# Query and key transfers split by groups of four heads, values from plain fp32, and a new order, in a transformer layer on one core

## The chip, the cores and the metric

The kernel runs on one core of one Trainium2 chip. The time is in device microseconds of one launch. The kernel before was timed in three runs: median 1072.35 us, 1069.49 to 1074.19.

A core has a matrix engine (PE, TensorE), a vector engine (DVE), a scalar engine (ACT) and GpSimd (POOL). Each works through its own list of instructions in order. SP (SyncE) computes nothing and issues transfers (DMAs). The engines wait for each other only by semaphores: an instruction that waits holds everything behind it on its engine.

## The reference

One layer of a vision tower on 8 images of 1024 tokens. 29 features are embedded into 128 channels and a table of positions is added. Then follow a layer norm, causal attention with 8 heads of 16 channels and a residual, and a second layer norm with a feed-forward part: a shared one and eight experts in two groups, of which each token takes two.

```python
def _L0_attn_ref(x, Wq, bq, Wk, bk, Wv, bv, Wo, bo):
    ...
    Q = split_heads(x @ Wq + bq)
    K = split_heads(x @ Wk + bk)
    V = split_heads(x @ Wv + bv)
    scores = jnp.einsum('bhqd,bhkd->bhqk', Q, K)
    causal = jnp.tril(jnp.ones((n, n), dtype=jnp.float32))
    mask = (1.0 - causal) * -100000.0
    attn = jax.nn.softmax((scores + mask) / math.sqrt(d), axis=-1)
    out = jnp.einsum('bhqk,bhkd->bhqd', attn, V)
    out = out.transpose(0, 2, 1, 3).reshape(b, n, c)
    return out @ Wo + bo
...
h = _L0_tok_ref(x, L0_tok_W)
h = h + _L0_attn_ref(_layernorm(h, axis=-1), ...)
h = h + _L0_ffn_ref(_layernorm(h, axis=-1), ...)
```

## The kernel before

**Split numbers.** Most fp32 products are made from a rounded part (`_h`, type fp32r) and its rest (`_l`), as three matmuls with fp32r operands: h*h, l*h and h*l (`split_mm`, L501 to L503). Some are plain fp32 matmuls, which the trace shows as two records each: embedding (L519), output projection (L623), gates (L633), and the weighing of the values (L598).

**Halves, units, passes.** An image has two halves of 512 tokens. The front of a half is: `emb` (embedding, then positions added by DVE), `stat1` (statistics on DVE and POOL), `turn1` (z turned by PE, L527; ACT copies the rounded part, `ztl` is DVE's subtraction), `q`, `k`, `v` (projections; ACT rounds, DVE subtracts, L747). All of these use one PSUM bank, `bank_m`.

Attention runs in four units of an image, (heads 0-3, half 0), (heads 4-7, half 0), (heads 0-3, half 1), (heads 4-7, half 1). Pass 1 makes every score (`score`, L553) and DVE takes row maxima from it (L767, L771). `turn` turns the maxima of a unit, DVE splits them and SP puts them as two more rows beside the queries (L470). Pass 2 (`prob`, L580) makes the scores again, the other way round and less the maximum; ACT takes the exponential (L1025), and `weigh` (L598) multiplies with the values. Scores and probs have two PSUM banks each.

**The stacks.** So that one matmul gives all three products of the split numbers, the 16 channels of a head stand three times in the rows of `q_stack` (h, h, l) and `k_stack` (h, l, h). They come there by transfers from SBUF to SBUF on SP's queue: six per half for the queries (L449) and six for the keys (L462), each 128 KB with all eight heads. The rows without channels hold zeros, and the keys' last two rows hold -1, against the maxima. The -1 are put in by eight small transfers at the beginning (`ones`). A half of `q_stack` is used by image after image, so the queries wait until the last `prob` of that half in the image before has been made:

```python
            def queries(i, half):
                sp.wait_ge(m_taken, after(i, "q", half))
                if i:
                    sp.wait_ge(st_ready, ((i - 1) * NP_ + HALF_P[half]) * G4)
```

**The order.** Each engine's list is woven from streams (scores, probs, weighing, middle, forward, combine, transfers) by strings of letters, one letter per step: `FIRST` for the start, `WEAVE` for each of six images in between, `LAST` for the end. In one period an engine makes probs of one image, the forward part of it and of the one before, and fronts and scores of the next. SP has the steps `queries` and `keys` of a half in its list, the maxima of the four units and the stores.

## Time and profile before

| | |
|---|---|
| median of 3 runs | 1072.35 us |
| profiled execution | 1073.58 us |
| its span | 1071.9 us |
| PE busy | 986.7 us (92%) |
| DVE busy | 777.3 us (73%) |
| ACT busy | 591.3 us (55%) |
| POOL busy | 322.1 us (30%) |
| transfers | 35.06 MB |

The span is one execution from its first to its last instruction. Busy time is a mean over stages that differ: at the beginning PE is nearly idle, in the middle it hardly ever is. A busy PE may still be slowed by its clock, which has two levels; the profile gives the granted one as a part of full speed. A time in brackets behind a row of the timeline is idle time of that engine just before, with the instruction or transfer that ended it. "PEld" is PE's loading of weights, which runs beside its matmuls.

### The profile page before, as it was taken

The numbers are of one execution on the slowest core, as the hardware profiler recorded it, in microseconds if no ns is written. First come the engines' busy times: TensorE is split into PE (matmuls) and PEld (weight loads), VectorE is DVE, ScalarE is ACT, GpSimd is POOL, SyncE is SP. The second block draws the span as 40 slices with busy tenths as digits, with TensorE's granted clock in tenths as the row PEclk, the third lists the DMA queues.
The fourth block names the chain that finished last, engine by engine and source line by source line (L and its number), as shares of the span: only waits on it lengthen the run. The fifth ranks groups of instructions, "written<-read, shape, count | busy, mean of one in ns | idle before, by whom it ended". The sixth has DMA issues, their size and how long they took to land.

```text
span 1071.9 us, 17016 instructions
## 1 busy us (share of the span) xinstructions
PE 986.7 (92%) x5552; PEld 665.1 (62%) x5552; DVE 777.3 (73%) x2444; ACT 591.3 (55%) x1351; POOL 322.1 (30%) x466
## 2 busy tenths in 40 slices
PE   2598999999999999999999998999989999899976
PEld 2354556676657666676667666666657676575554
DVE  6478758885788857986688857987588858788233
ACT  2034655566554665557545765647655665446734
POOL 3031313324232223324142333323142242322334
PEclk9999999999999999999999999999999999899989
DMA  3540045003140045002350053100550041300000
GB/s 118 69 56 2 10 53 74 1 2 50 34 63 2 2 72 74 1 2 31 43 73 1 2 72 49 26 1 3 71 72 2 1 64 33 45 2 1 12 1 20
DMA packets 29480, 35.06 MB, mean 33 GB/s; under 512 B 5696, under 2 KB 15936, under 8 KB 29264
## 3 DMA queue, kind: packets, MB, share of 16 engines
q1 hardware_dynamic: 29392, 33.97, 21.5%
q8 instruction: 45, 0.74, 0.3%
q14 instruction: 43, 0.35, 0.1%
HBM read 4.02 MB, written 4.19 MB: 8 GB/s over the span
## 4 chain that ended last, share of the span: by engine, by line
PE 75%; DVE 9%; DMA 4%; ACT 3%; SPq 3%; issue 3%; POOL 2%; ACTq 0%; POOLq 0%; DVEq 0%
PE bank_p L580 14%; PE bank_s L553 13%; PE bank_w L598 11%; PE bank_f L679 5%; PE bank_f L680 5%; PE bank_f L681 5%; DMA q_stack<-qk_l 3%; PE bank_m L645 3%; PE bank_f L501 2%; SPq L449 2%; PE bank_f L503 2%; PE bank_f L502 2%; DVE mx_far L767 2%; PE bank_m L501 2%; ACT pt L1025 1%
## 5 line engine op out<-in xcount | busy, mean ns | idle before, releaser
L1025 ACT ACTIVATE pt<-bank_p 128x512 f32<-128x512 f32 (+3 forms) x768 | 350.0, 491 | 266.0 <-PE bank_p L580 260.6
L553 PE MATMUL bank_s<-k_stack,q_stack 112*128 112x512 f32 (+3 forms) x768 | 273.4, 394 | 36.3 <-DMA q_stack<-qk_l 12.5
L771 DVE CUSTOM_DVE_ANT_0 bank_s<-bank_s,causal 128x384 f32<-128x384 f32 (+3 forms) x512 | 246.0, 507 | 65.2 <-PE bank_s L553 60.7
L580 PE MATMUL bank_p<-q_stack,k_stack 128*128 128x512 f32 (+3 forms) x768 | 256.4, 379 | 5.3 <-ACT pt L1025 4.2
L553 PEld LDWEIGHTS bank_s<-k_stack,q_stack 112*128 112x128 f32 x768 | 146.9, 197 | 140.1 <-DVE mx L771 58.0
L767 DVE TENSOR_REDUCE mx_far<-bank_s 128x1 f32<-128x512 f32 x256 | 166.8, 684 | 35.2 <-PE bank_s L553 33.5
L1166 POOL TENSOR_SCALAR_AFFINE_SELECT pt<-pt 128x512 f32<-128x512 f32 x128 | 81.8, 639 | 361.0 <-ACT pt L1025 361.0
L580 PEld LDWEIGHTS bank_p<-q_stack,k_stack 128*128 128x128 f32 x768 | 138.9, 193 | 77.6 <-ACT pt L1025 48.7
L598 PE MATMUL bank_w<-pt,v 128*32 128x512 f32 (+3 forms) x1536 | 159.3, 497 | 0.6 <-POOL pt L1166 0.5
L679 PE MATMUL bank_f<-wex_h,hid_h 128*128 128x512 f32 x256 | 103.2, 403 | 0.1
L681 PE MATMUL bank_f<-wex_h,hid_l 128*128 128x512 f32 x256 | 101.2, 395 | 0.0
L680 PE MATMUL bank_f<-wex_l,hid_h 128*128 128x512 f32 x256 | 101.2, 395 | 0.0
L1198 POOL TENSOR_TENSOR sel<-sel 128x256 f32<-128x256 f32 x64 | 47.2, 737 | 145.3 <-ACT sel L1087 144.9
L1087 ACT ACTIVATE sel<-sel,wsel 128x128 f32<-128x128 f32 x256 | 81.4, 394 | 12.3 <-DVE sel L935 11.7
L1081 ACT ACTIVATE sel<-bank_f,gm 128x512 f32<-128x512 f32 x64 | 44.1, 688 | 58.6 <-PE bank_f L681 48.4
L771 DVE DVE_READ_ACCUMULATOR2_ANT mx<- 128x1 f32 x512 | 72.6, 142 | 0.0
L935 DVE SCALAR_TENSOR_TENSOR sel<-bank_f,gm,sel 128x512 f32<-128x512 f32 x64 | 47.7, 745 | 30.5 <-PE bank_f L681 27.9
L598 PEld LDWEIGHTS bank_w<-pt,v 128*32 128x32 f32 x1536 | 32.7, 108 | 55.0 <-issue 35.2
L501 PE MATMUL bank_f<-z2t_h,win_h 128*128 128x512 f32 x128 | 54.7, 428 | 2.5 <-DVE gate L916 1.8
L679 PEld LDWEIGHTS bank_f<-wex_h,hid_h 128*128 128x128 f32 x256 | 48.2, 188 | 11.0 <-issue 2.8
L681 PEld LDWEIGHTS bank_f<-wex_h,hid_l 128*128 128x128 f32 x256 | 48.1, 188 | 11.3
L680 PEld LDWEIGHTS bank_f<-wex_l,hid_h 128*128 128x128 f32 x256 | 48.5, 190 | 8.8
(130 smaller groups left out, 1351.5 us busy)
## 6 DMA issues: line engine op xcount, KB each, us to landing
q_stack<-qk_h SPq DMA_DIRECT2D x64, 128.0 KB, 3.9
k_stack<-qk_h SPq DMA_DIRECT2D x64, 128.0 KB, 5.8
q_stack<-qk_l SPq DMA_DIRECT2D x32, 128.0 KB, 5.2
k_stack<-qk_l SPq DMA_DIRECT2D x32, 128.0 KB, 5.9
out<-h SPq DMA_DIRECT2D x16, 256.0 KB, 4.3
x_sb<-x_t SPq DMA_DIRECT2D x16, 64.0 KB, 5.7
pt<-w_expert SPq DMA_DIRECT2D x1, 1024.0 KB, 5.6
pos_sb<-pos SPq DMA_DIRECT2D x2, 256.0 KB, 3.1
```

What stands on the lines that cost most here:

```text
L501: nc.tensor.matmul(dst, wh, xh, start=True, stop=False)
L553: nc.tensor.matmul(s_bank[s % 2][:, 0:cols], q_stack[0:STACK, half, hd, t % HT * P:(t % HT + 1) * P], k_stack[0:STACK, hd // 2, key_place( ...
L580: nc.tensor.matmul(p_bank[p % 2][:, q0:HALF], k_stack[:, hd // 2, key_place(i, kt // HT), kt % HT * P:(kt % HT + 1) * P], q_stack[:, half, ...
L598: mm = nc.tensor.matmul(w_bank[VW * j:VW * (j + 1), q0:HALF], v[:, i % 2, kt, first:first + VW], pt[:, k % PT_SLOTS, j, q0:HALF], start=(k ...
L679: nc.tensor.matmul(f_bank[g][:], hid_h[:, c, tok], wex_h[:, c, w], start=(c == 0), stop=False)
L680: nc.tensor.matmul(f_bank[g][:], hid_h[:, c, tok], wex_l[:, c, w], start=False, stop=False)
L681: mm = nc.tensor.matmul(f_bank[g][:], hid_l[:, c, tok], wex_h[:, c, w], start=False, stop=(c == HID // P - 1))
L767: nc.vector.tensor_reduce(mx_far[:, u, col:col + 1], s_bank[s % 2][:], AX.X, ALU.max).then_inc(s_taken, 1)
L771: nc.vector.tensor_tensor_reduce(src, src, causal[:, HALF - cols:HALF], 1.0, -3.0e38, ALU.add, ALU.max, mx[:, u, col:col + 1]).then_inc(s_ ...
L1025: nc.scalar.activation(pt[:, k % PT_SLOTS, j, q0:HALF], p_bank[p % 2][:, q0:HALF], ACT.Exp, scale=0.25).then_inc(exp_done, 1)
L1087: nc.scalar.mul(sel[:, t % 2, part], sel[:, t % 2, part], wsel[:, t, e:e + 1]).then_inc(weighted, 1)
L1166: nc.gpsimd.affine_select(out=d, in_=d, compare_op=ALU.is_ge, fill=0.0, base=0, pattern=[[0, G4], [1, P]], channel_multiplier=-1).then_inc ...
```

## The change

The change has four parts, and a new set of orders that goes with them.

1. **Transfers by groups.** Queries and keys go to their stacks by groups of four heads: six transfers of 64 KB for each of queries and keys, half and group, so 48 per image and not 24. Each group has its own semaphore, and a score waits for its unit's group alone. A group's queries wait only until the `prob` steps of their own unit in the image before are through (`UNIT_LAST`).
2. **The keys' stack is filled with -1** in all its rows, once, and the queries' stack with zeros; the product of the unused rows stays zero. The eight small transfers go. ACT fills half 0 of the queries and the first place of the keys, POOL the rest.
3. **A shorter beginning.** DVE clears only x_sb (in halves) and mx. Positions are loaded on ACT's queue. Weights of queries and keys come first, those for the output projection and the feed-forward part are loaded behind the first half's stacks (`load_rest`), into other tiles than before (`gate`, `hid`, and no more `pt`). Weights are split behind z.
4. **Values from plain fp32.** ACT also copies the turned z unrounded, back into `z`; one fp32 matmul per tile of 128 tokens takes the place of three. The next half's z waits for them.

```diff
-    moves = [("queries", 0), ("keys", 0), ("queries", 1), ("keys", 1)]
+    moves = [(what, half, g) for half in range(2) for g in range(2) for what in ("queries", "keys")]
 FIRST = {
     "pe": (
-        "mmmmmmmdmssssdsssssmsmsmssmsssmssssssmssmssssssppsspsssppsspspmspsdppsppspswsswppdsswsppspspswss"
...
+        "mmmmmdmmmmmmssdssmmssssssssssssssmsmsssssssssssppsspspssspmspdswspsppsdpssspsppsswppssppspssswss"
...
-            def queries(i, half):
+            def queries(i, half, g):
 
                 sp.wait_ge(m_taken, after(i, "q", half))
                 if i:
-                    sp.wait_ge(st_ready, ((i - 1) * NP_ + HALF_P[half]) * G4)
+                    sp.wait_ge(st_ready, ((i - 1) * NP_ + UNIT_LAST[2 * half + g] + 1) * G4)
                 for n, part in enumerate((qk_h, qk_h, qk_l)):
                     for odd in range(2):
                         to = slice(odd * ODD + n * DH, odd * ODD + (n + 1) * DH)
-                        rows = part[odd * (P // 2):(odd + 1) * (P // 2), 0, :]
-                        sp.dma_start(words(q_stack[to, half, odd::2, :]), words(rows)).then_inc(q_in[half], 16)
+                        sp.dma_start(words(q_stack[to, half, g * G4 + odd:(g + 1) * G4:2, :]),
+                                     group_rows(part, 0, odd, g)).then_inc(q_in[half][g], 16)
...
+                if (i, half, g) == (0, 1, 0):
+                    sp.wait_ge(other_keys_made, 1)
...
                     keys(i, st[1], st[2])
                     if st[2] and i < B - 1:
                         load_x(i + 1, st[1])
+                    if i == 0 and st == ("keys", 0, 1):
+                        load_rest()
...
                 if kind == "v":
...
-                        mm = split_mm(m_bank[:, tok], zt_h[:, tok], zt_l[:, tok], wqkv_h[:, 2, :], wqkv_l[:, 2, :])
+                        mm = nc.tensor.matmul(m_bank[:, tok], z[:, t, :], wv_sb[:], start=True, stop=True)
...
-                if s == UNIT_S0[0] or s == UNIT_S0[2]:
-                    pe.wait_ge(q_in[half], (i + 1) * 96)
-                if s == UNIT_S0[0] or s == UNIT_S0[2] + ROWS:
-                    pe.wait_ge(k_in[half], (i + 1) * 96)
+                if s == UNIT_S0[u]:
+                    pe.wait_ge(q_in[half][g], (i + 1) * 96)
+                if s == UNIT_S0[u] + half * ROWS:
+                    pe.wait_ge(k_in[half][g], (i + 1) * 96)
...
-                        dve.wait_ge(m_ready, after(half_before(i, half)[0], "turn1", 1 - half))
+                        dve.wait_ge(m_ready, after(half_before(i, half)[0], "v", 1 - half))
...
-                dve.wait_ge(zth_made, n + 1)
+                dve.wait_ge(zt_made, n + 1)
...
-            nc.vector.memset(x_sb[XROWS:ODD, :, :], 0.0).then_inc(x_padded, 1)
-            nc.vector.memset(x_sb[ODD:P, :, :], 0.0).then_inc(x_padded, 1)
-            nc.vector.memset(words(k_stack[:, 0:2, :, :]), 0.0).then_inc(keys_zeroed, 1)
-            nc.vector.memset(words(k_stack[:, 2:, :, :]), 0.0).then_inc(stacks_zeroed, 1)
-            nc.vector.memset(words(minus1), -1.0).then_inc(minus1_made, 1)
+            for half in range(2):
+                nc.vector.memset(x_sb[XROWS:ODD, half, :], 0.0).then_inc(x_padded, 1)
+                nc.vector.memset(x_sb[ODD:P, half, :], 0.0).then_inc(x_padded, 1)
...
                     nc.scalar.copy(zt_h[:], m_bank[:]).then_inc(zth_made, 1)
+                    nc.scalar.copy(z[:].rearrange("p t c -> p (t c)"), m_bank[:]).then_inc(zt_made, 1)
...
+                    if i == 0 and st == ("q", 0):
+                        act.wait_ge(blank_made, 2)
+                        nc.scalar.copy(k_stack[:, :, 0, :], blank[:, 1:2].unsqueeze(2).to_broadcast([P, HEADS // 2, HALF])).then_inc(first_keys_made, 1)
...
             def constants():
+                pool.wait_ge(z_made, HT)
...
+                nc.gpsimd.memset(words(k_stack[:, :, 1:3, :]), -1.0).then_inc(other_keys_made, 1)
```

How the lists move, at three places. First DVE at the very beginning, before (`wqkv` are the three projections' weights, `bank_m` is the embedding at its first use):

```order
L983 MEMSET x_sb 32x1024
L984 MEMSET x_sb 64x1024
L985 MEMSET k_stack 128x3072
L986 MEMSET k_stack 128x3072
L987 MEMSET hid_l 2x1024
L988 MEMSET mx 128x512
L718 TENSOR_TENSOR h<-bank_m,pos_sb 128x512
L724 BN_STATS stats<-h 128x6 x4
...
L947 CAST wqkv_h<-z 128x128 x3
L950 TENSOR_TENSOR wqkv_l<-z,wqkv_h 128x128 x3
L736 TENSOR_SCALAR z<-h,mv,rs 128x128 x4
```

and the same of the changed kernel:

```order
L990 MEMSET x_sb 32x512
L991 MEMSET x_sb 64x512
...
L992 MEMSET mx 128x512
L723 TENSOR_TENSOR h<-bank_m,pos_sb 128x512
L729 BN_STATS stats<-h 128x6 x4
...
L741 TENSOR_SCALAR z<-h,mv,rs 128x128 x4
L952 CAST wqk_h<-z 128x128 x2
L955 TENSOR_TENSOR wqk_l<-z,wqk_h 128x128 x2
L747 TENSOR_TENSOR zt_l<-bank_m,zt_h 128x512
```

The two memsets of the keys' stack and the one for the -1 are gone from ahead of h (those of x_sb stand twice), and the weights' split stands behind z.

Second SP where the second half's queries of an image in the middle are sent, before (`mrow` are the rows of maxima, `st_ready` counts probs):

```order
L449 DMA q_stack<-qk_h 16x4x512 [waits st_ready,m_bank_taken]
L449 DMA q_stack<-qk_h 16x4x512 x3
L449 DMA q_stack<-qk_l 16x4x512 x2
L470 DMA q_stack<-mrow_h 1x16x128 [waits m_bank_taken]
L470 DMA q_stack<-mrow_l 1x16x128
L462 DMA k_stack<-qk_h 16x4x512 [waits st_ready,m_bank_taken]
L462 DMA k_stack<-qk_h 16x4x512
L462 DMA k_stack<-qk_l 16x4x512 x2
```

and of the changed kernel, from the same queries on:

```order
L449 DMA q_stack<-qk_h 16x2x512 [waits st_ready,m_bank_taken]
L449 DMA q_stack<-qk_h 16x2x512 x3
L449 DMA q_stack<-qk_l 16x2x512 x2
L474 DMA q_stack<-mrow_h 1x16x128 [waits m_bank_taken]
L474 DMA q_stack<-mrow_l 1x16x128
L474 DMA q_stack<-mrow_h 1x16x128 [waits m_bank_taken]
L474 DMA q_stack<-mrow_l 1x16x128
L465 DMA k_stack<-qk_h 16x2x512 [waits st_ready,m_bank_taken]
L465 DMA k_stack<-qk_h 16x2x512
L465 DMA k_stack<-qk_l 16x2x512 x2
```

The maxima of units 0 and 1 now both stand ahead of the half's first keys, and behind these (not shown) follow the second group's queries and keys.

Third PE at the beginning, from the first values' projection on, before (`bank_s` holds scores):

```order
L501 MATMUL bank_m<-wqkv_h,zt_h 128x128 [waits m_bank_taken]
L502 MATMUL bank_m<-wqkv_h,zt_l 128x128
L503 MATMUL bank_m<-wqkv_l,zt_h 128x128
...
L553 MATMUL bank_s<-k_stack,q_stack 128x128 [waits keys_in_stack_0,queries_in_stack_0]
...
L553 MATMUL bank_s<-k_stack,q_stack 128x256 [waits scores_taken] x4
L553 MATMUL bank_s<-k_stack,q_stack 128x384 [waits scores_taken] x2
```

and of the changed kernel:

```order
L544 MATMUL bank_m<-wv_sb,z 128x128 [waits m_bank_taken,w_values_loaded]
L544 MATMUL bank_m<-wv_sb,z 128x128 x3
L531 MATMUL bank_m<-ident,z 128x128 [waits m_bank_taken,z_made]
...
L559 MATMUL bank_s<-k_stack,q_stack 128x128 [waits keys_in_stack_0_0,queries_in_stack_0_0]
...
L505 MATMUL bank_m<-zt_h,wqk_h 128x512 [waits m_bank_taken]
...
L559 MATMUL bank_s<-k_stack,q_stack 128x256 [waits scores_taken] x4
```

Four matmuls stand for the twelve of the values, the second half's z is turned ahead of the first score, and its projections follow the first four scores.

## Rows read from the trace of the kernel before

**Rows 1.** Busy time by stretch: start, length, busy us per engine, clock, DMA.

```profile
30.00:40.00 10.00, 1.61 (x8) 1.42 (x7) 2.97 (x13) 0.00 (x0) 1.28 (x2) 1.00 0.98 113
...
426.10:549.00 122.90, 119.38 (x696) 81.67 (x695) 95.12 (x306) 72.97 (x169) 38.38 (x56) 0.99 0.23 33
```

**Rows 2.** PE's waits: instruction, releaser, us in total, times, longest.

```profile
PE bank_s L553 <- DMA q_stack<-qk_l: 12.5, 7, 2.7
...
PE bank_s L553 <- DMA k_stack<-qk_h: 8.7, 1, 8.7
```

**Rows 3.** Timeline of the beginning: start, us, engine, line, operation, [idle before].

```profile
3.30 2.04 PE L519 MATMUL bank_m<-tokw_sb,x_sb 128*128 128x128 f32 x8 [3.30 <-DVE x_sb L984]
...
3.85 2.62 DVE L985 MEMSET k_stack<- 128x3072 f32 x1 [0.70 <-issue]
...
11.21 0.62 DVE L718 TENSOR_TENSOR h<-bank_m,pos_sb 128x512 f32<-128x512 f32 x1
...
14.74 3.01 DVE L947 CAST wqkv_h<-z 128x128 fp32r<-128x128 f32 x3
...
18.49 1.10 DVE L736 TENSOR_SCALAR z<-h,mv,rs 128x128 f32<-128x128 f32 x4
...
25.49 2.60 SPq L449 DMA_DIRECT2D q_stack<-qk_h  x4
...
31.99 1.25 SPq L462 DMA_DIRECT2D k_stack<-qk_h  x2
...
40.31 0.66 PE L553 MATMUL bank_s<-k_stack,q_stack 112*128 112x128 f32 x2 [8.70 <-DMA k_stack<-qk_h]
```

**Rows 4.** Timeline where images change: queries' rest, last prob, transfers, wait, score.

```profile
404.88 0.75 DVE L747 SCALAR_TENSOR_TENSOR qk_l<-bank_m,bq_sb,qk_h 128x512 fp32r<-128x512 f32 x1
...
413.54 0.34 PE L580 MATMUL bank_p<-q_stack,k_stack 128*128 128x128 f32 x2
...
413.95 2.47 SPq L449 DMA_DIRECT2D q_stack<-qk_h  x4
...
416.47 1.24 SPq L449 DMA_DIRECT2D q_stack<-qk_l  x2
...
420.66 0.33 PE L566 MATMUL bank_m<-ident,mx 128*128 128x128 f32 x1
...
422.83 0.94 PE L553 MATMUL bank_s<-k_stack,q_stack 112*128 112x512 f32 x2 [1.84 <-DMA q_stack<-qk_l]
```

**Rows 5.** Timeline of PE, the same wait in three later images.

```profile
545.50 0.77 PE L553 MATMUL bank_s<-k_stack,q_stack 112*128 112x512 f32 x2 [1.59 <-DMA q_stack<-qk_l]
...
791.89 0.73 PE L553 MATMUL bank_s<-k_stack,q_stack 112*128 112x512 f32 x2 [1.64 <-DMA q_stack<-qk_l]
...
913.97 0.73 PE L553 MATMUL bank_s<-k_stack,q_stack 112*128 112x512 f32 x2 [1.98 <-DMA q_stack<-qk_l]
```

**Rows 6.** Busy time by stretch, just behind two of these waits.

```profile
423.00:425.00 2.00, 2.00 (x7) 1.22 (x8) 1.29 (x2) 0.38 (x1) 1.33 (x3) 0.55 1.07 127
...
792.00:794.00 2.00, 1.89 (x10) 1.25 (x10) 1.50 (x3) 0.65 (x2) 1.60 (x3) 1.00 1.09 125
```

**Rows 7.** Timeline of PE: one half's values, one half's embedding, and what follows each.

```profile
369.40 1.05 PE L519 MATMUL bank_m<-tokw_sb,x_sb 128*128 128x128 f32 x8
...
370.21 0.54 PE L580 MATMUL bank_p<-q_stack,k_stack 128*128 128x384 f32 x2
...
383.45 0.33 PE L501 MATMUL bank_m<-wqkv_h,zt_h 128*128 128x128 f32 x1
...
384.85 0.67 PE L580 MATMUL bank_p<-q_stack,k_stack 128*128 128x512 f32 x2
```

**Rows 8.** Groups of instructions: count, busy us, mean ns, idle before.

```profile
L1001 ACT CAST zt_h<-bank_m 128x512 fp32r<-128x512 f32 x16 | 9.4, 585 | 29.9 <-PE bank_m L527 29.4
```

**Rows 9.** Transfers: tile, queue, count, KB each, median us to landing.

```profile
k_stack<-qk_h SPq DMA_DIRECT2D x64, 128.0 KB, 5.8
...
q_stack<-mrow_h SPq DMA_DIRECT2D x32, 8.0 KB, 1.8
```

More of the change, by code:

```diff
@@ L323, in build @@
         z2, z2t = sb("z2", [P, HT, P]), sb("z2t", [P, HALF])
-        wq_sb, wk_sb, wv_sb = (z2[:, n, :] for n in range(3))
+        wq_sb, wk_sb = (z2[:, n, :] for n in range(2))
         z2t_h, z2t_l = sb("z2t_h", [P, HALF], F32R), sb("z2t_l", [P, HALF], F32R)
@@ L440, in queries, with group_rows @@
-            def queries(i, half):
+            for dst, src in ((wv_sb, wv), (bv_sb, bv), (bo_sb, bo)):
+                sp.dma_start(dst[:], src).then_inc(wv_in, 16)
+            sp.wait_ge(queries_zeroed, 2)
+            sp.wait_ge(first_keys_made, 1)
+            def group_rows(part, w, odd, g):
+                first = odd * (P // 2) + g * (P // 4)
+                return words(part[first:first + P // 4, w, :])
+            def queries(i, half, g):
                 sp.wait_ge(m_taken, after(i, "q", half))
@@ L460, in keys @@
                         to = slice(odd * ODD + n * DH, odd * ODD + (n + 1) * DH)
-                        rows = part[odd * (P // 2):(odd + 1) * (P // 2), 1, :]
-                        sp.dma_start(words(k_stack[to, :, key_place(i, half), :]), words(rows)).then_inc(k_in[half], 16)
+                        sp.dma_start(words(k_stack[to, 2 * g:2 * g + 2, key_place(i, half), :]),
+                                     group_rows(part, 1, odd, g)).then_inc(k_in[half][g], 16)
             def maxima(i, u):
@@ L967, in stage @@
                     front(i, st)
+                    if i == 0 and st == ("turn1", 0):
+                        split_front_weights()
                 elif kind == "ztl":
@@ L1004, in front @@
                     if n:
-                        act.wait_ge((q_in, k_in)[w][1 - half], ((n - 1) // 2 + 1) * 96)
+                        for g in range(2):
+                            act.wait_ge((q_in, k_in)[w][1 - half][g], ((n - 1) // 2 + 1) * 96)
+                    if n == 0:
+                        act.wait_ge(wqk_in, 4 * 16)
                     nc.scalar.activation(qk_h[:, w, :], m_bank[:], ACT.Identity,
@@ L1093, in split_forward_weights @@
                 nc.scalar.copy(wex_h[:], wex_sb).then_inc(wsplit_h, 1)
-                act.wait_ge(wsplit_l, 2)
             def stage(i, st):
-                if i == 0 and st == ("prob", 0, 0):
-                    split_forward_weights()
+                if i == 0 and st == ("in", 0, 0):
+                    act.wait_ge(wsplit_l, 2)
+                if i == 0 and st == ("turn", 0):
+                    round_forward_weights()
                 if st[0] == "prob":
@@ L1108, in stage @@
                     post(i, st)
-            act.wait_ge(keys_zeroed, 1)
-            zeros = words(k_stack[:, 0, :, :])
-            for n in range(0, HEADS, 2):
-                nc.scalar.copy(q_stack[:, 1, n:n + 2, :], zeros[:, 0:2, :]).then_inc(stacks_zeroed, 1)
-            act.wait_ge(w_in1, 7 * 16)
+            for half in range(2):
+                act.dma_start(pos_sb[:, tiles(half), :], pos[:, tiles(half), :]).then_inc(pos_in[half], 16)
+            act.wait_ge(blank_made, 1)
+            nc.scalar.copy(q_stack[:, 0, :, :], blank[:, 0:1].unsqueeze(2).to_broadcast([P, HEADS, HALF])).then_inc(queries_zeroed, 1)
             for i, st in PROGRAM["act"]:
```

234 lines of the change are left out of this document (113 added, 121 removed).

## The prediction

> **What bounds the kernel now.** I read the busy time by stretch first. Between two equal places of consecutive images (426.1 to 549.0) PE is busy 119.4 of 122.9 us, DVE 95.1, ACT 73.0 [rows 1]. So in the steady part the order of instructions on PE sets the pace, and what counts is PE work and the few places where PE stands still. In the stretch 30 to 40 us PE is busy 1.6 us while the DMA engines are at 0.98 [rows 1]: the beginning is bound by something else. PE's waits say what [rows 2]: 12.5 us in seven waits for the low parts of the queries (`q_stack<-qk_l`), once per image, and 8.7 us once for the first keys. These are the two largest. The timelines of the two places [rows 3, 4] then show which instruction is late, and why.
>
> **The beginning.** In before the first score starts at 40.31 [rows 3]. Followed back: the last of the 12 stack transfers is issued at about 32.6 (31.99 plus half of 1.25), the first at 25.49; the queries behind them stand on z at 18.49, which stands behind the three weight casts at 14.74, and h at 11.21 stands behind the two memsets of k_stack (the first at 3.85, 2.62 us) although its matmuls were done at 5.34 (3.30 + 2.04). After the change, step by step:
> - DVE has four half-size memsets of x_sb and one of mx ahead of h: by the row of the k_stack memset (3072 columns in 2.62 us) 2560 columns, about 2.2 us and five starts, so it is free before 5 us. h waits for PE only: 5.4 instead of 11.21, gain 5.8. The positions now come by ACT's queue at the very start, so they don't hold it.
> - The weights are split behind z and not ahead of it: 18.49 - 14.74 = 3.75 us leave the chain. z starts near 18.49 - 5.8 - 3.75 = 8.9. Two thirds of those 3.75 us (two weights, not three) fill the 2.5 us in which PE turns z and ACT copies, so the low part of zt is ready for its turn, or up to 1 us late.
> - ACT's added copy of zt stands between: +0.59, by its twin at 0.585 [rows 8].
> - SP must also wait for the -1 in the first keys' stack: 2048 columns on ACT behind the first queries. its copy of 512 columns takes 0.585 [rows 8], so at most 2.3 us and, with one start in place of four, about 2.0; the queries' low part takes 0.8 of that beside it, so 1.2 is added.
> Sum for the first issue: 25.49 - 5.8 - 3.75 + 0.59 + 1.2 = 17.7. Then SP issues 6 queries' and 6 keys' transfers of group 0. One issue costs 0.62 (1.24 for two [rows 4]) whatever its size: the 8 KB rows of the maxima aren't cheaper. 12 issues, 7.5 us: 25.2. In before the same 12 carried 128 KB each and landed 7 us after the last issue; 1.57 MB from 25.49 to 40.3 is 106 GB/s, the pace at which the engines stand full [rows 1]. With 64 KB each, 0.79 MB at that pace is 7.4 us, as long as the issuing, so the last lands 2 to 5 us behind its issue (8 KB takes 1.8, 128 KB 5.8 [rows 9]); I take 3.5. First score at 28.8, gain 11.5. Bounds: 5 (only the memsets leave, casts held by GpSimd's memsets, which now start at the same moment) to 14. The work behind it is the same and shifts with it.
>
> **The values.** Split, one half's values are 12 matmuls from 383.45 to 384.85, 1.40 us. Plain fp32, four tiles of the same 128x128 shape are the embedding: eight records from 369.40 to 370.21, 0.81 us [rows 7]. 0.59 less for each half. 14 halves outside the beginning: 8.2. They stand in PE's order between dependent work, so the gain is full where PE is never idle (97%). Bounds 4 to 10.
> On plain fp32 the Trainium skill (FP8 and Floating Point Precision, TensorE Precision Notes) says that it takes four passes through the array. By that rule alone four tiles are 16 passes against 12 for the split, 1.40 x 16/12 = 1.87, a loss of 0.47 per half and 1057 for the whole. The trace has the four tiles at 0.81: here the split pays more than one pass for each of its short matmuls. The row decides; the rule is a rival below.
>
> **The wait per image.** Rows 4 have it whole. The queries of the second half were finished by DVE at 405.63, but SP issues them at 413.95, right behind the last `prob` (413.54 + 0.34), because the stack's half is only free when all of the image before has been read. Six issues, landing at 422.8; PE ran dry at 420.99 and waited 1.84. After the change the transfer of group 0 waits for unit 2 only, which `prob` leaves a whole unit of 32 steps earlier; it can start at 405.6 plus the 0.6 of ACT's copy, and lands by 406.2 + 3.7 + 5.8 = 415.7 even at the old landing time, 5 us before PE comes. Group 1 still waits for the last `prob`, but its first score is 32 scores on. So 12.5 us in seven waits go. What is late next: the maxima's two rows for the first `prob`, which now stand ahead of the half's keys, and DVE's two score buffers; neither has a row near 1 us per image.
> Behind five of the seven waits TensorE's granted clock falls to about half (0.55 in 423 to 425: the 1.2 GHz level) and behind others it stays at 1.00 (792 to 794) [rows 6]. From 422.83 to 545.50 (with the fall) are 122.67, from 791.89 to 913.97 (without) 122.08 [rows 4, 5]: a fall costs 0.6. With the wait gone, five falls: 3. Together 15.5; bounds 6 (the gap is filled by the next dependency) and 18.
>
> **What is added.** ACT gets 14 more copies of 0.585 us [rows 8], 8.2 us on an engine at 59%. Each can push an exp that PE waits for; nothing on ACT is idle-free, so I take about a third, +3; bounds 0 and 8.2. SP issues 48 stack transfers per image, not 24: 24 x 0.62 = 14.9 us more, on a queue that was quiet for most of an image. What stands behind them are the maxima and the next image's x. I take +2; bounds 0 and the rival below. The bytes stay the same. Rows 9 have 1.8 us to landing for 8 KB and 5.8 for 128 KB in a full queue, so most of the 5.8 is queueing, and half the bytes should land earlier. The Trainium skill (DMA: Bandwidth & Descriptors, Rules for kernel authors) speaks against cutting transfers up: two transfers to disjoint partition halves share the same 16 engines and serialize, so one should be used. By that rule the first group's landing would gain nothing from its size, 3 us of the beginning would come back, and the whole would be 1045; by the rows it is 1042. The new orders themselves I count 0, bounds -8 and +8: the row order at the seams is nearly the old one.
>
> **Sum.** 1071.9 (span) - 11.5 - 8.2 - 15.5 + 3 + 2 = 1041.7. The profiled execution took 1073.58, 1.7 over its span, and so would be 1043.4; the median of the runs, 1072.35, is 1.2 below it. I forecast 1042.
>
> **Rivals.**
> - *Other waits take the place.* The seam wait is half refilled (6.2 back), the clock falls partly stay (1.6) and ACT's copies cost their full length (5.2 more): 1042 + 13 = 1055. For it: PE, DVE and ACT all wait on each other through pairs of buffers, and PE's 97% leaves little other slack. Against: rows 4 show the wait at a place where DVE and ACT had nothing in flight for PE.
> - *The late load.* The remaining weights (2 MB by their shapes) are now issued behind the first half's stacks and ahead of the second half's. At 106 GB/s that is 19 us of transfers, and the second half's queries queue behind them. If they come 10 us late, most of the gain of the beginning is lost: 1052. Against: 32 scores lie between, over 20 us at DVE's pace there.
> - *Four passes decide*: the values get dearer, 1057, as worked out above.
> - *Better orders.* The orders were bound by the late queries; freed of them they lose several small waits more, 2 us per image: 1028.
> - *Slower.* SP becomes the bound once per image: the rows of maxima stand behind a group's 12 issues (7.4 us), and PE's first `prob` of the unit waits all of it, with a fall of the clock: 8.0 x 7 = 56, 1098. It decides from 30/7 = 4.3 us per image on. For it: SP's issues are doubled, and they are in one line. Against: in before SP issues nothing for most of each image, and the maxima go ahead of the second half's keys.
>
> **How the numbers follow.** Forecast 0.60 (own range 1034 to 1049); other waits 0.15; late load 0.08; four passes 0.03; better orders 0.09; slower 0.05. The range takes in better orders to 1028 and the rivals up to 1057, with some room for the unknown price of the queue: 1027 to 1060 leaves out about 0.15. Within 0.5% (5.4 us, about what a measurement of this kernel tells from no change) needs two of the gains to fail together: 0.04, out of the ends of "other waits" and "slower". So faster 0.92, same 0.04, slower 0.04.
>
> **What would show it.** First score near 29 us. The values' group at 0.8 us per half. No wait of PE for `q_stack<-qk_l` over 0.5 us in the steady images, the granted clock at 1.00 through their seams, and an image every 120 us instead of 122.5. SP's queue with 48 stack issues per image of 0.6 us. It is wrong if the waits for the maxima (`mrow_l`) or for `k_stack` come up by more than 1 us per image, if an image still takes 122, or if the first score is later than 34.

## The result and the profile after

The changed kernel takes 1024.14 us (median of 4 runs, 1021.18 to 1025.72) against 1071.74 us for the kernel before, measured beside it (4 runs). The ratio is 0.9556, 95% interval 0.9538 to 0.9575: 47.6 us faster. The forecast was 1042 with a range from 1027 to 1060. The direction was right and the size too small; the measured time lies 3 us below the range.

The busy time between two equal places of consecutive images in the changed kernel, and a stretch where the image changes (start and length, busy us and instructions of PE, PE's weight loads, DVE, ACT, POOL; granted clock; share and GB/s of the DMA engines):

```profile
405.30:521.90 116.60, 115.30 (x687) 79.47 (x686) 94.11 (x305) 73.50 (x170) 38.41 (x56) 1.00 0.13 34
...
395.00:405.00 10.00, 9.78 (x60) 6.25 (x54) 8.78 (x21) 8.29 (x21) 5.78 (x9) 1.00 0.15 38
```

An image takes 116.6 us where it took 122.9 [rows 1]. PE is busy 4.1 us less and idle 2.2 us less. The DMA engines are busy 0.13 of the time, not 0.23, for the same bytes. PE's longest waits in the changed kernel:

```profile
PE bank_p L585 <- ACT pt L1033: 9.2, 29, 0.6
PE bank_m L531 <- DVE z L741: 6.6, 2, 4.7
PE bank_s L559 <- DVE mx L776: 4.9, 13, 1.5
PE bank_m L523 <- DMA tokw_sb<-tok_w: 4.6, 1, 4.6
```

No wait for a stack transfer is left; the two largest of before [rows 2] are gone. What is left in the steady images is many waits of 0.3 us for ACT's exponentials (9.2 us in all; 4.2 in before). The beginning, as a timeline (start, us, engine, line, operation, and the idle time before it):

```profile
4.59 2.08 PE L523 MATMUL bank_m<-tokw_sb,x_sb 128*128 128x128 f32 x8 [4.59 <-DMA tokw_sb<-tok_w]
...
6.79 0.69 DVE L723 TENSOR_TENSOR h<-bank_m,pos_sb 128x512 f32<-128x512 f32 x1 [2.75 <-PE bank_m L523]
...
10.39 1.10 DVE L741 TENSOR_SCALAR z<-h,mv,rs 128x128 f32<-128x128 f32 x4
...
18.87 2.60 SPq L449 DMA_DIRECT2D q_stack<-qk_h  x4
...
25.31 1.23 SPq L465 DMA_DIRECT2D k_stack<-qk_h  x2
...
27.92 1.11 PE L531 MATMUL bank_m<-ident,z 128*128 128x128 f32 x4 [4.67 <-DVE z L741]
28.69 0.67 PE L559 MATMUL bank_s<-k_stack,q_stack 112*128 112x128 f32 x2
```

The first score starts at 28.69, where it was 40.31 [rows 3] and the forecast had 28.8. It is not the keys' transfers that hold it here: the new order puts the turn of the second half's z ahead of it on PE, and PE waits 4.67 us for that z. With the old orders (experiment 1) the first score does wait for the keys, and starts at 28.27. The place where images change, which answers to [rows 4]:

```profile
383.78 3.79 SPq L449 DMA_DIRECT2D q_stack<-qk_h  x4
...
387.61 1.23 SPq L449 DMA_DIRECT2D q_stack<-qk_l  x2
...
395.42 0.44 PE L585 MATMUL bank_p<-q_stack,k_stack 128*128 128x128 f32 x2
...
398.14 0.48 PE L559 MATMUL bank_s<-k_stack,q_stack 112*128 112x512 f32 x1
```

The queries go out 12 us ahead of the half's last `prob` (395.42), not behind it. The score that needs them starts 2.7 us after the start of that `prob`; in before PE came to it 7.4 us after (413.54 to 420.99). So the new order brings it closer, and that only works because the queries are released early. Values and transfers, beside [rows 7] and [rows 9]:

```profile
362.41 1.05 PE L544 MATMUL bank_m<-wv_sb,z 128*128 128x128 f32 x8
...
363.22 0.48 PE L684 MATMUL bank_f<-wex_h,hid_h 128*128 128x512 f32 x1
```

```profile
q_stack<-qk_h SPq DMA_DIRECT2D x128, 64.0 KB, 2.2
k_stack<-qk_h SPq DMA_DIRECT2D x128, 64.0 KB, 2.3
```

One half's values take 0.81 us, as forecast. A 64 KB transfer lands in 2.2 to 2.3 us; 128 KB took 5.8. None of the five falls of the granted clock behind the seam waits is left. One fall of 3.4 us (882 to 885.4) stands elsewhere in the steady images, with no listed wait of PE over 0.5 us in the 10 us before it.

### The profile page after: what moved, and what is told of

The parts are those of the page before. It is cut to its first block, busy times and chain, and to the rows that moved or that the text cites. A ratio compares the mean times of both kernels' runs of the same rounds, so it can differ in the third digit from the quotient of the medians.

```text
span 1022.1 us, 17138 instructions
## 1 busy us (share of the span) xinstructions
PE 965.0 (94%) x5488; PEld 647.8 (63%) x5488; DVE 763.6 (75%) x2441; ACT 599.1 (59%) x1365; POOL 325.3 (32%) x469
## 4 chain that ended last, share of the span: by engine, by line
PE 83%; DVE 8%; ACT 4%; issue 2%; POOL 1%; DMA 0%; ACTq 0%; POOLq 0%; DVEq 0%; SPq 0%
PE bank_p L585 15%; PE bank_s L559 14%; PE bank_w L603 13%; PE bank_f L684 6%; PE bank_f L685 6%; PE bank_f L686 6%; PE bank_f L505 3%; PE bank_m L650 3%; PE bank_f L507 3%; PE bank_f L506 3%; ACT pt L1033 2%; DVE mx_far L772 2%; PE bank_m L523 2%; PE bank_m L618 1%; PE bank_m L544 1%
## 5 line engine op out<-in xcount | busy, mean ns | idle before, releaser
L559 PE MATMUL bank_s<-k_stack,q_stack 112*128 112x512 f32 (+3 forms) x768 | 270.5, 385 | 8.2 <-DVE mx L776 4.9
L559 PEld LDWEIGHTS bank_s<-k_stack,q_stack 112*128 112x128 f32 x768 | 144.8, 194 | 98.9 <-DVE mx L776 45.1
L603 PE MATMUL bank_w<-pt,v 128*32 128x512 f32 (+3 forms) x1536 | 161.6, 498 | 0.5 <-POOL pt L1181 0.3
L940 DVE SCALAR_TENSOR_TENSOR sel<-bank_f,gm,sel 128x512 f32<-128x512 f32 x64 | 47.6, 744 | 26.3 <-PE bank_f L686 14.6
L1071 ACT ACTIVATE gate<-bank_f 128x512 f32<-128x512 f32 x64 | 38.5, 602 | 28.7 <-PE bank_f L507 28.6
```

The source lines that it names most:

```text
L559: nc.tensor.matmul(s_bank[s % 2][:, 0:cols], q_stack[0:STACK, half, hd, t % HT * P:(t % HT + 1) * P], k_stack[0:STACK, hd // 2, key_place( ...
L603: mm = nc.tensor.matmul(w_bank[VW * j:VW * (j + 1), q0:HALF], v[:, i % 2, kt, first:first + VW], pt[:, k % PT_SLOTS, j, q0:HALF], start=(k ...
```

## The experiments

Each was timed beside the kernel before, on the same chip as it (the median of before was 1070.4 to 1072.3). "Old orders" are the strings of before, with each transfer step `d` written twice because there are now two groups. The differences between two variants below are differences of medians; taken from the ratios to before instead, they come out up to 1.4 us otherwise, so a difference of 2 us or less between two numbers is hardly one.

**1. Old orders.** The changed kernel with the three tables of before:

```
-        "spsmspspmspspmppssmspswsppwpssm ...     (WEAVE, pe)
+        "sspmpssmppssmppssmcppwspsscppmw ...     (before, 'd' -> 'dd', all engines)
```

> The changed kernel with the letters of the kernel before (each step of the transfers' stream doubled, since there are now two groups). Forecast was 1042, measured 1024. Theory A (orders): what I missed is the small waits that the new orders save, some 2 us per image and the tail; then this runs 12 to 20 us over the changed kernel, 1036 to 1044. Theory B (the wait per image was mis-sized, because the clock falls and the scores behind it are slowed too): the old orders keep nearly all of the gain, at most 5 us over, 1024 to 1029, and still show no wait for q_stack<-qk_l.

Measured 1039.37 us, ratio 0.9709 (0.9693 to 0.9725). That is the size of theory A: the orders are worth 15.2 us of the 47.6. The rest, 1039.4, is within 3 us of a forecast that had counted the orders at nothing. An image takes 118.9 us here. The first score waits for the keys in this order:

```profile
28.27 0.66 PE L559 MATMUL bank_s<-k_stack,q_stack 112*128 112x128 f32 x2 [5.04 <-DMA k_stack<-qk_h]
```

**2. New orders alone.** The kernel before with the tables of the changed one, half of the transfer steps dropped, and POOL's split of the forward weights three steps later (an outline of the edit, not its text):

```
+FIRST, WEAVE, LAST of the changed kernel, four 'd' of eight
-                if i == 0 and st == ("prob", 0, 0):
+                if i == 0 and st == ("prob", 0, G4 - 1):
```

> The kernel before with the letters of the changed one (of the eight transfer steps of an image the four that send the first group's share now send the whole; GpSimd's split of the forward weights is put three steps later, since it would be in its own way). Theory A: 1052 to 1060, most small waits gone. Theory B: 1068 to 1080; the queries are still sent only behind the last prob, and orders alone don't help, or harm.

Measured 1139.92 us, ratio 1.0651 (1.0628 to 1.0673): 69 us slower than before, as neither expected. PE's first waits:

```profile
PE bank_s L553 <- DMA q_stack<-qk_l: 39.4, 7, 6.9
PE bank_s L553 <- issue: 21.6, 7, 3.2
```

and the stretch at the end of one of them:

```profile
454.00:458.00 4.00, 2.97 (x8) 2.17 (x9) 1.38 (x2) 0.60 (x1) 0.00 (x0) 0.50 1.07 143
```

The order that gains 15 us with early queries loses 69 with late, large ones: 5.6 us per image at one seam, 3.1 at the other, and a clock of 0.50 behind the waits. The 3.1 are at the first half's first score, behind the sending of that half's keys; the profile names no releaser there (`issue`), so that these are the keys is an inference.

**3. Split values again.**

```
-  mm = nc.tensor.matmul(m_bank[:, tok], z[:, t, :], wv_sb[:], start=True, stop=True)
+  mm = split_mm(m_bank[:, tok], zt_h[:, tok], zt_l[:, tok], wqk_h[:, 2, :], wqk_l[:, 2, :])
-  nc.scalar.copy(z[:].rearrange("p t c -> p (t c)"), m_bank[:]).then_inc(zt_made, 1)
```

> The changed kernel with the values again from three split matmuls per tile and without ACT's added copy. By my term, 0.59 us per half for 14 to 16 halves, less what ACT's copies cost: +5 to +9, 1029 to 1033. If the copies cost nothing: +8 to +10. Theory C (the values were mis-sized, since their end holds bank_m and everything behind it): +15 or more.

Measured 1029.35 us, ratio 0.9618 (0.9599 to 0.9636): plain values less ACT's copies are worth 5.2 us (6.6 by the ratios), near the forecast's 8.2 - 3.

**4. Late release, new orders.**

```
-  sp.wait_ge(st_ready, ((i - 1) * NP_ + UNIT_LAST[2 * half + g] + 1) * G4)
+  sp.wait_ge(st_ready, ((i - 1) * NP_ + HALF_P[half]) * G4)      (queries only)
```

> The changed kernel, but a group's queries wait until the last prob of their half in the image before, as before; transfers still by groups of 64 KB. Theory A: the wait comes back at its old price of 1.5 to 2.2 us per image less the faster landing, +7 to +12, 1031 to 1036. Theory B: 4 to 5 us per image with the fall of the clock, +25 or more, 1050. If nothing comes back (under +3), the smaller transfers alone had removed the wait and the early release is worth nothing.

Measured 1057.88 us, ratio 0.9879 (0.9858 to 0.9901): 33.7 slower than the changed kernel, the size of theory B. Its seam:

```profile
405.92 0.44 PE L585 MATMUL bank_p<-q_stack,k_stack 128*128 128x128 f32 x2
...
406.43 2.46 SPq L449 DMA_DIRECT2D q_stack<-qk_h  x4
...
408.94 1.23 SPq L449 DMA_DIRECT2D q_stack<-qk_l  x2
...
411.85 0.80 PE L559 MATMUL bank_s<-k_stack,q_stack 112*128 112x512 f32 x1 [2.95 <-DMA q_stack<-qk_l]
```

Six issues and one landing are 5.9 us (405.92 to 411.85); the new order leaves 2.7, so PE waits 2.95, and the clock falls behind each of its seven seams (for 3.4 or 6.8 us). An image takes 122. Listed waits for transfers are 18.5 us in six images and 4.3 for the rows of maxima; the rest of the 33.7 was not split up, and the lower clock is a candidate for it.

**5 and 6. Late release, old orders; and with split values too.** Experiments 1 and 4 together, then 3 as well:

```
 (5) orders of before, 'd' -> 'dd', and
-  ... UNIT_LAST[2 * half + g] + 1) * G4)
+  ... HALF_P[half]) * G4)
 (6) and besides
-  matmul(m_bank[:, tok], z[:, t, :], wv_sb[:], ...)
+  split_mm(m_bank[:, tok], zt_h[:, tok], zt_l[:, tok], wqk_h[:, 2, :], wqk_l[:, 2, :])
```

> The changed kernel with the orders of before (each of the four transfer steps written twice) and, besides, the queries' transfers of both groups waiting for the last prob of the whole half of the image before, as in before. So of the change at the seam only the size of the transfers (64 KB for 128 KB) and their order by groups are left. It differs from the second run kernel (old orders, early release, 1039.4 us) in the release alone. In before the last prob of a half ends 7.4 us ahead of the first score that needs the new queries, and six transfers took 8.9 us from first issue to the last landing: 1.84 us of waiting. With 64 KB the landing is 2.2 instead of 5 or more, 6 x 0.62 + 2.2 = 5.9 us, under 7.4. Theory 'size': the wait goes by the smaller transfers alone, 1039 to 1043, no wait for q_stack<-qk_l over 0.5 us per image. Theory 'release' (the forecast's words: the wait goes because group 0 may be overwritten a whole unit earlier): the wait stays near 1.8 us with a clock fall of 0.6, so 1039.4 + 7 x 2.1 = 1054, at least 1050.

> As the kernel before it in this call, and with the split values of before too (twelve fp32r matmuls per half, no added ACT copy, weights of the values split). Against the kernel of before it has the new beginning and the 64 KB transfers, nothing else. Forecast's own sizes: values net of ACT's copies are worth 5.2 with the new orders, so 5 more than e5_old_orders_late: 1044 to 1048 by theory 'size', 1057 to 1060 by theory 'release'. A rival says that values are worth less with the old orders (PE stands idle more there): 2 to 4 more only.

Measured 1062.44 us (ratio 0.9926, 0.9908 to 0.9944) and 1067.92 (0.9968, 0.9957 to 0.998). The 1062 is above even theory "release", whose sum was 1054, and the 1068 above its 1057 to 1060. By the trace of number 5 neither theory was right. The values are worth 5.5 us here, and not the 2 to 4 of the rival. The wait for `q_stack<-qk_l` is gone with late release, so 64 KB is enough for it, but another stands in its place:

```profile
405.02 2.47 SPq L449 DMA_DIRECT2D q_stack<-qk_h  x4
...
407.53 1.23 SPq L449 DMA_DIRECT2D q_stack<-qk_l  x2
...
408.86 1.19 SPq L465 DMA_DIRECT2D k_stack<-qk_h  x2
...
412.63 0.59 SPq L474 DMA_DIRECT2D q_stack<-mrow_h  x1
413.26 0.59 SPq L474 DMA_DIRECT2D q_stack<-mrow_l  x1
...
415.17 0.50 PE L585 MATMUL bank_p<-q_stack,k_stack 128*128 128x512 f32 x1 [2.65 <-DMA q_stack<-mrow_l]
```

Late queries push the keys behind them on SP, and the keys push the two rows of maxima that the next `prob` reads. This is the mechanism of the forecast's "slower" rival, at 2.8 us per image (19.9 in seven waits).

Numbers 1, 4 and 5 with the changed kernel give the orders' worth under both releases: 15.2 us with early queries (1039.4 to 1024.1) and 4.6 with late ones (1062.4 to 1057.9). The gain is not the orders' alone.

**7. Rows of maxima first.** Number 5 with one letter of SP's WEAVE string moved:

```
-        "spsfpddpsppsssmmmcssfpwddmwpwc"
+        "spsfpdpsppsssmmmdcssfpwddmwpwc"
```

> The kernel with old orders and late release of the queries (1062.4 us) with one letter moved in SP's repeated block: the six transfers of the first group's keys of the second half now stand behind the rows of maxima that the first prob reads, not ahead of them. In its trace PE waited for those rows (q_stack<-mrow_l) 2.65 us in each image, 19.9 in seven waits, with a clock fall of 3.4 us in six seams, and no longer for q_stack<-qk_l. Theory 'queue' (the late queries cost only by what SP's line puts behind them): the rows are issued 3.7 us earlier, the wait and the falls go in the six images of the block, 1062.4 - 6 x 3.3 = 1043, 1040 to 1048. Theory 'release' (with the queries issued behind the last prob something is late whatever the line): the wait goes over to the first group's keys or the second group's queries, 1056 or more.

Measured 1041.24 us, ratio 0.9718 (0.9704 to 0.9731). Theory "queue" holds, within 2 us of its sum: one letter is 21.2 us. In its trace the rows follow the queries at once, and the `prob` does not wait:

```profile
403.43 1.24 SPq L449 DMA_DIRECT2D q_stack<-qk_l  x2
...
404.71 0.59 SPq L474 DMA_DIRECT2D q_stack<-mrow_h  x1
405.34 0.59 SPq L474 DMA_DIRECT2D q_stack<-mrow_l  x1
...
408.26 0.39 PE L585 MATMUL bank_p<-q_stack,k_stack 128*128 128x512 f32 x1
```

One wait of 2.0 us for these rows is left, at 170.05, in the first block, whose string was not changed. With this line the old orders lose 1.9 us at most by the late release (1.0 by the ratios), which is hardly a difference. Early release, which the forecast made the cause of the whole gain at the seam, is one of two ways to get it there. With the new orders the late release cost 33.7 us (number 4); whether another line of SP would mend that too was not tried.

**8. Whole transfers.** The changed kernel's beginning and values with the six 128 KB transfers (and the row pattern that goes with them), the late release and the undoubled orders of before:

```
-  sp.dma_start(words(q_stack[to, half, g * G4 + odd:(g + 1) * G4:2, :]), group_rows(part, 0, odd, g))
+  sp.dma_start(words(q_stack[to, half, odd::2, :]), group_rows(part, 0, odd))     (keys alike)
```

> The changed kernel with its beginning and its plain values, but with the stack transfers of before: six of 128 KB for a half's queries and six for its keys, the queries waiting for the last prob of the half, and the orders of before. So it differs from the kernel with 64 KB transfers and one letter moved (1041.2 us), and from that with the queries released early (1039.4), in the transfers alone; and from before in the beginning and the values. Theory 'transfers' (the forecast's sum with the seam's term left out): the wait of 1.8 us for q_stack<-qk_l and the fall of the clock come back in seven seams, 7 x 2.4 = 17, and the first score comes 2 to 4 us later than 28.3, so 1041 + 17 + 3 = 1061, 1057 to 1064; against before that is a beginning of 8 and values of 3 to 5. Rival: the seam was closed by something else in the changed kernel (ACT and DVE no longer in each other's way), and the wait stays under 0.5 us: 1041 to 1046.

Measured 1070.37 us (12 runs), ratio 0.9994 (0.9979 to 1.0009): 29.1 us above number 7, 9 more than I expected, and equal to before. Two rows of PE show where time is lost here:

```profile
393.23 0.41 PE L558 MATMUL bank_s<-k_stack,q_stack 112*128 112x128 f32 x2 [0.85 <-issue]
...
421.36 0.73 PE L558 MATMUL bank_s<-k_stack,q_stack 112*128 112x512 f32 x2 [1.97 <-DMA q_stack<-qk_l]
```

The second is the old wait, unchanged. The first is one that has grown: the last of the half's keys go out at 386.25 to 387.5 and take 6.1 us to land (median); the values stand between, so what PE saves there it can lose in waiting. In before PE had been busy throughout ahead of the same score in this image, and stood still for 0.4 to 0.6 us in the six others:

```profile
PE bank_s L553 <- issue: 2.7, 6, 0.6
```

In number 8 that row has 6.7 us in seven waits, the longest 1.2, and in number 9, with slower values, 3.7 in six. So 3.0 us of the values' 8.2 are seen to go there. The profile names no transfer as releaser of these waits; that it is the keys' landing is read from the positions. The first score starts at 34.41, and image 1's embedding only 1.6 us earlier than before (118.6 against 120.2).

**9. Whole transfers and split values**: number 8 with number 3's edit, that is, the kernel before with the new beginning alone:

```
-  matmul(m_bank[:, tok], z[:, t, :], wv_sb[:], ...)
+  split_mm(m_bank[:, tok], zt_h[:, tok], zt_l[:, tok], wqk_h[:, 2, :], wqk_l[:, 2, :])
```

> The kernel with whole-half transfers of 128 KB, late release and old orders (1070.4 us) with the split values of before too. So it is before with the new beginning alone. With whole transfers PE waited 2.0 us for q_stack<-qk_l and 0.85 behind the first half's keys, and the first half's values stand between the issue of these keys and the score that waits for them. Theory 'eaten': one of the two halves' gain ends in that wait, the other is kept and ACT's copies cost it again, so values are worth 0 to 2 here: 1070 to 1073. Rival 'constant': the values are worth 5.2 as with the new orders and 64 KB: 1074 to 1077, above before.

Measured 1072.28 us, ratio 1.0004 (0.9993 to 1.0016). The number is where "eaten" had it: values are worth 1.9 us here and 5.2 to 5.5 elsewhere. The new beginning alone is worth nothing that can be measured: its first score is at 33.22, 7.1 us earlier, but image 1's embedding is 3.0 earlier and the last image's 1.0. Which waits take the rest was not followed up.

**10. Two copies.** ACT's copy of zt into z made twice.

```
+                    act.wait_ge(zt_made, n + 1)
+                    nc.scalar.copy(z[:].rearrange("p t c -> p (t c)"), m_bank[:]).then_inc(zt_twice, 1)
```

> The changed kernel with ACT's added copy of the turned half into z made twice, one after the other, and the low part of zt waiting for the second. It prices the term 'ACT copies +3' of the forecast: 15 or 16 more copies of 0.585 us on ACT. Theory 'part': the copy pushes an exp that PE waits for in about a third of the cases, +3 us (1027). Theory 'free but for the beginning': ACT is 59% busy and the low part of zt is not waited for in the steady images, so only the one in the beginning is paid, +0.6 to +1.3, within 1024 to 1026. Upper bound: every copy paid twice on the chain (copy and the low part behind it), +9 to +18.

Measured 1027.48 us, ratio 0.9594 (0.9578 to 0.9611): +3.3 (4.1 by the ratios), near the forecast's +3. PE's waits for ACT's exponentials grew from 9.2 us (29) to 11.8 (35).

**11. A shorter start.**

```
+            sp.dma_start(tokw_sb[:], tok_w)  ahead of  load_x(0, 0)
-            sp.wait_ge(first_keys_made, 1)    (SP's first queries no longer wait for the -1)
+                    if i == 0 and st == ("k", 0):
+                        first_keys()          # six transfers issued by ACT, not by SP
```

> The changed kernel with a shorter beginning: the token weights loaded ahead of x, the first keys' six transfers of the first group issued by ACT and not behind the queries' on SP, and SP's first queries no longer waiting for the -1 in the keys' stack. In the changed kernel the embedding waited for the token weights to 4.59 (3.3 in the kernel before), SP issued its first queries at 18.87 (their high part was there at 17.0), the last of the keys at 25.9, and the first score started at 28.69. Theory 'the beginning is serial and everything behind it shifts': 1.3 (weights) and 1.7 to 2.3 (keys, ready at 21.06, six issues of 0.62), first score near 25.5 and 1021 in all. Rival: the first half is bound by DVE's maxima or by the second half's queries, 32 scores on, and the earlier score is given back: 1023 to 1024.

Measured 1022.59 us, ratio 0.9548 (0.9535 to 0.9561), which overlaps the changed kernel's: no gain to be told. Its first score is at 29.36, later than 28.69. ACT had issued the last of these keys by 25.0, but transfers were on the way from two queues at once. Transfers of its first 30 us:

```profile
q_stack<-qk_l SPq DMA_DIRECT2D x4, 64.0 KB, 3.6
k_stack<-qk_h ACTq DMA_DIRECT2D x4, 64.0 KB, 3.9
```

They landed in 2.2 to 2.3 in the changed kernel's first 30 us. Two queues shared the same engines, which were full from 24 us on; besides, SP sent the second group's queries 5 us sooner (21.59 for 26.58). So what was saved in issuing was lost in landing. On this the Trainium skill (DMA: Bandwidth & Descriptors, Rules for kernel authors) agrees: transfers to disjoint partitions share the same 16 engines from one queue or from two. There was little to win besides: ahead of the first score stands the second half's turn, which waited for its z until 27.74 here and 27.92 in the changed kernel, and the wait for the keys behind it is 0.50. The token weights gave 0.15 us, since x then landed last.

**12 to 15. Where the orders' gain hangs.** The changed kernel with old orders in the first block alone (12), in the repeated block alone (13), in the repeated block for PE, DVE and ACT alone (14), and there for DVE alone (15). The edits in outline:

```
+FIRST = before's        | +WEAVE = before's      | +WEAVE["pe","dve","act"] | +WEAVE["dve"]
```

> The changed kernel with the old order in the first block alone (image 0 and its overlap), new orders in the repeated block and the last. The new orders are worth 15.2 us in all (1039.4 against 1024.1). Images take 118.9 with the old and 116.8 with the new, six of them: 12.6; that leaves 2.6 for the beginning and the end. Theory 'steady': 1025 to 1028. Rival: the gain lies in the first images (second period 123.8 against 120.0): 1028 to 1033.

> The changed kernel with the old order in the repeated block alone. Theory 'steady': six images lose 2.1 us each, 1034 to 1038. Rival (the gain lies in the first images): 1027 to 1031. If old and new blocks don't fit each other at their ends, both this and the kernel before it in this call are slower than these sums.

> The changed kernel with the old orders of PE, DVE and ACT in the repeated block, and the new orders of SP and POOL there. All five old in that block gave 1036.3 us, 12.2 over the changed kernel; an image took 118.9 in place of 116.8, 1.8 of the 2.4 between the starts of scores on PE. Theory 'fit of PE and DVE' (the new order sets each score where DVE has its buffer free): the same loss, 1034 to 1039. Rival 'queue' (the new order of SP, which puts a group's rows of maxima ahead of the transfers that follow): the loss goes, 1024 to 1028.

> The changed kernel with DVE's old order alone in the repeated block. Theory 'fit': PE and DVE pass score buffers to each other in turn, and an order of DVE that was drawn up for another order of PE makes PE wait more than both old orders together do: over 1036, 1040 to 1080. Rival 'PE alone' (what counts is where PE's scores stand between other work; DVE catches up through its two buffers): 1024 to 1030.

Measured 1026.67 us, 1036.28, 1036.76 and 1080.33 (ratios 0.959, 0.9682, 0.9682 and 1.0089, each within 0.0026). The first two, +2.5 and +12.1, add up to 14.7 of the 15.2: most of the gain is in the steady images, and the two parts add. The clock has no part in it: its mean is 0.996 in number 13 and 0.995 in the changed kernel. SP's and POOL's orders in the repeated block have none either (1036.76 against 1036.28). DVE's old order with the new ones of the others is 56 us slower, so what counts is the fit of DVE's order to the others'. PE's waits with DVE's order alone old:

```profile
PE bank_s L559 <- DVE mx L776: 17.2, 32, 1.5
PE bank_s L559 <- DVE mx_far L772: 7.7, 9, 1.1
PE bank_f L684 <- DVE gate L921: 7.2, 7, 1.1
```

The first two are score buffers; the third is the feed-forward part, so the misfit is not in the scores alone.

## Why the prediction was off, point by point

The variants form a ladder from before to after, which shows what each part is worth where it stands (medians from several chips, between which before itself moved by up to 1.9 us):

| step | median us | difference |
|---|---|---|
| before | 1071.7 | |
| + beginning (9) | 1072.3 | 0 |
| + plain values (8) | 1070.4 | -1.9 |
| + transfers by groups, 64 KB, but keys now ahead of maxima (5) | 1062.4 | -8.0 |
| + maxima ahead of keys in SP's line (7) | 1041.2 | -21.2 |
| queries released early, SP's line as in 5 (1) | 1039.4 | -1.9 |
| + new orders (after) | 1024.1 | -15.2 |

- **The orders** are the step that failed: "The new orders themselves I count 0, bounds -8 and +8: the row order at the seams is nearly the old one." They are worth 15.2 us with the queries released early, nearly twice the bound. With -15.2 for 0 the forecast's sum is 1026.5, within 2.4 us of the median; that the other terms come out so well together is partly luck (see the beginning and the wait per image). I read the seams alone; the gain is spread over the scores. From the start of a score to the start of what follows it on PE, an image of number 1 spends 24.0 us on its scores and one of the changed kernel 22.3, and that is 1.8 of the 2.3 us between 118.9 and 116.6 (from the starts of PE's instructions in one image of each). The waits for DVE's release of a score buffer (`mx_far`) were 6.8 us in number 1 and 1.3 in the changed kernel:

```profile
PE bank_s L559 <- DVE mx_far L772: 6.8, 13, 0.7
PE bank_s L559 <- DVE mx L776: 5.5, 16, 0.9
```

```profile
PE bank_s L559 <- DVE mx_far L772: 1.3, 4, 0.4
```

  So the traces show where the time went, and number 15 that DVE's order matters; that the handing over of score buffers is all of the cause is not shown. The rival "better orders" had the size per image (2 us, 1028 in all) and the small waits; it was given 0.09.
- **The beginning**: first score 28.69 for 28.8, by the steps named (h at 6.79 and not 5.4, because the token weights came last, 4.59; z at 10.39 for 8.9). That the position came out to 0.1 us is luck: the twelve issues ended at 26.54 and not at 25.2; the keys were there some 1.7 us later (by the 28.27 of number 1, an estimate) and not 3.5; and the new order then put another instruction ahead of the score. As a term of the sum it was too large: image 1's embedding came 8.9 us earlier in the changed kernel, 8.4 in number 1, not 11.5.
- **The values**: 0.81 us for a half, net 5.2 with ACT's copies at 3.3. Right in all three numbers, as far as the runs can tell. By the Trainium skill (FP8 and Floating Point Precision, TensorE Precision Notes) plain fp32 takes four passes through the array. Priced at the split's time per matmul that gave the estimate of 1.87 us; the row after has 0.81, and the rival built on that price fell.
- **The wait per image**: it went, and was worth more than counted. From number 7 to number 8 the whole-half transfers cost 29.1 us: 3.5 us in each image (118.9 to 122.4, so 21 to 24 in all) and 6.2 at the first score (28.17 to 34.41). The forecast's 15.5 covered one seam; the other, with keys landing 6.1 us after issue, was mostly hidden behind the slower values and showed in before as 2.7 us in six small waits, which the forecast did not use. In number 1 all but the orders is 32.3 us; less 8.4 for the beginning and 5.2 for the values, some 19 are left for the seams (an estimate by subtraction), where the forecast had 15.5 - 2. This shortfall and the excess at the beginning largely cancel. The cause given (early release) is one of two that suffice with the old orders; with the new ones nothing else was tried.
- **SP's queue** (+2): 48 issues at 0.62 us each were there. In the changed kernel no wait of PE for any of them is listed; with late queries and the line of number 5 they cost 21 us. The rival "slower" was a real mechanism that the early release keeps away.
- **The terms are not a sum.** Beginning and values, 16.7 us in the forecast with ACT's copies, gave 1 us with whole transfers. A gain ahead of a transfer that sets the pace is given back in the wait for it; for the values 3.0 us of this are seen in the waits, for the beginning it is an inference.
- **The other rivals.** "Late load" did not come: PE has no wait for a transfer behind the first one at 4.6 us. "Other waits" came in part: those for ACT's exponentials grew from 4.2 to 9.2 us.

## What to carry to other kernels

Where an order is drawn up anew together with a release, price the two together (here 15.2 us with the early release, 4.6 with the late one): measure how far behind the release the order now puts the first user (7.4 us before, 2.7 after), and count what the order can win over all waits of the steady part, not at the seam. In a line of transfers, ask for each who waits behind it: two 8 KB rows behind six key transfers cost 21 us. Count on the gains of different steps to add only where no transfer between them sets the pace.

## What the runs showed of the hardware

- Landing depends on size and on what is in flight more than in proportion: 64 KB from SP's queue alone 2.2 to 2.3 us, 128 KB 4.1 to 6.1 (medians, number 8), 64 KB from two queues together 3.6 to 3.9. The same bytes kept the 16 engines busy 0.23 of the time in pieces of 128 KB and 0.13 in pieces of 64 KB. The copies' partition and row pattern changed with the groups too, and no run here tells that from the size.
- Behind some single waits of PE at a seam the granted clock fell to the lower level, the 1.2 GHz one: in before behind five of seven (0.55 to 0.59 in the 2 to 4 us behind), in number 2 behind waits of 6 us (0.50). The length of the wait alone does not tell which: in number 8 it fell behind one of 1.54 us (0.66 from 788 to 792) and not behind one of 1.97 (1.00 from 421 to 425). Once it fell with no such wait: in the changed kernel, 882 to 885.4, the longest idle time of PE that the timeline lists in the 10 us before was 0.45. In the kernel with DVE's old order PE waited 32 times for one releaser, 17.2 us in all, the longest 1.5, and its clock stayed at the upper level (1.00) through all the steady images.
